# A two-layer post-LN decoder on one core: chunked context reload, a moved key-difference step, per-tile LayerNorm signals and a rebuilt last stage

## The reference

```python
x = ln(x + L0_attn(x))    # linear attention, 16 heads
x = ln(x + L0_xattn(x, ctx))   # softmax attention, 8 heads of 64, over 6404 context rows
x = ln(x + L0_ffn(x))     # mixture of 64 experts, 2 shared ones
x = ln(x + L1_attn(x))    # one softmax head over the 1024 tokens
x = ln(x + L1_xattn(x, ctx))
x = ln(x + L1_ffn(x))

# L1_xattn: every linear layer quantises its input to int8 by its largest magnitude
i_scale = max(max|x|, 1e-8) / 127
out = (clip(round(x / i_scale), -128, 127) @ qW.T) * (w_scale * i_scale) + b
vis, image_embeds = linear(ctx), linear(vis)      # from the context alone
... two attention rounds give `fused` ...
h = relu(linear([fused, mean(image_embeds)], W_f1)); result = linear(h, W_f2)

# L1_ffn: 8 low-rank experts of rank 64, two of them chosen by token 0 for all tokens
gates = softmax over the top 2 of x[0] @ Wr.T
result = x + sum_e gates[e] * (x @ A[e].T) @ Bw[e].T
```

## Time and profile before

| what | us |
|---|---|
| three runs | 1777.51, 1777.84, 1782.12 |
| median | 1777.84 |
| the profiled execution, as timed | 1776.72 |
| its span in the profile | 1775.0 |
| granted TensorE clock, mean | 0.911 of 2.4 GHz |
| layer 0's cross-attention (first exponential to the end of its norm) | 158.3 to 1091.7 |
| pair 3, of this | 884.8 to 1078.4 |
| mixture of experts | to 1328.7 |
| layer 1's cross-attention, first to last exponential | 1460.5 to 1694.1 |
| from its last exponential to the end | 1694.1 to 1775.0 |

### The profile page before, as it was taken

How to read it: one execution, slowest core, us unless ns; L and a number is a source line. 1 busy time by engine, 2 the same in 40 slices (tenths; PEclk the granted TensorE clock), 3 DMA queues, 4 the chain that set the end, 5 groups by cost and what they waited for, 6 DMA issues and landing times.

```text
span 1775.0 us, 26171 instructions
## 1 busy us (share of the span) xinstructions
PE 1532.3 (86%) x8928; PEld 551.9 (31%) x8928; DVE 1289.4 (73%) x2241; ACT 1122.0 (63%) x1495; POOL 424.5 (24%) x411
## 2 busy tenths in 40 slices
PE   3778889999999999999979997999987679968944
PEld 2412223333333333333322323334334413212313
DVE  4698678778787778877759897666655576877764
ACT  4687666776876767867647785555553367655532
POOL 5401333343433334423300010344440000000000
PEclk7957889999999999999989997999997759968967
DMA  4000000000000000000020000111100000000000
GB/s 123 7 0 6 1 1 1 1 1 7 1 1 1 1 1 3 1 1 1 1 58 1 1 1 25 36 43 41 44 13 1 1 1 1 1 0 1 1 1 24
DMA packets 11869, 20.28 MB, mean 11 GB/s; under 512 B 1558, under 2 KB 11046, under 8 KB 11558
## 3 DMA queue, kind: packets, MB, share of 16 engines
q1 hardware_dynamic: 11750, 18.76, 3.9%
HBM read 18.23 MB, written 0.52 MB: 11 GB/s over the span
## 4 chain that ended last, share of the span: by engine, by line
PE 53%; issue 17%; DVE 17%; ACT 7%; POOL 4%; DMA 2%; ACTq 0%; POOLq 0%; SPq 0%; DVEq 0%
PE PS L1704 21%; PE PS L1689 13%; DVE KNB L1049 5%; POOL WRK L575 4%; PE PS L1736 3%; DVE WRK L1099 3%; PE PS L1652 2%; ACT KNB L729 2%; ACT WRK L709 2%; PE PS L1579 2%; DMA KNB<-in_ctx_fm_dram 1%; DVE QS L1105 1%; ACT KB L630 1%; PE PS L1978 1%; DVE KB L979 1%
## 5 line engine op out<-in xcount | busy, mean ns | idle before, releaser
L1099 DVE TENSOR_TENSOR WRK<-WRK 128x768 f32<-128x768 f32 (+1 forms) x500 | 545.0, 1090 | 56.9 <-ACT WRK L709 45.3
L709 ACT ACTIVATE WRK<-PS 128x1024 f32<-128x1024 f32 (+1 forms) x510 | 497.4, 1023 | 105.9 <-PE PS L1689 91.5
L1704 PE MATMUL PS<-WRK,V 128*64 128x512 f32 (+1 forms) x2040 | 498.4, 609 | 0.0
L1049 DVE CUSTOM_DVE_ANT_0 KNB<-PS,KNB 128x512 f16<-128x512 f32 (+2 forms) x464 | 330.9, 730 | 120.1 <-PE PS L1736 108.0
L548 POOL TENSOR_TENSOR WRK<-WRK 128x256 f32<-128x256 f32 x300 | 269.8, 899 | 426.7 <-ACT WRK L709 406.9
L729 ACT ACTIVATE KNB<-PS 128x512 f16<-128x512 f32 (+2 forms) x306 | 181.0, 591 | 121.9 <-PE PS L1736 121.6
L1874 PE MATMUL PS<-WRK,KNB 128*128 128x512 f16 x828 | 196.4, 382 | 11.0 <-POOL WRK L575 4.3
L1689 PE MATMUL PS<-Q,KB 64*128 64x512 f16 (+1 forms) x1428 | 192.3, 381 | 11.3 <-ACT WRK L709 11.2
L1704 PEld LDWEIGHTS PS<-WRK,V 128*64 128x64 f32 (+1 forms) x2040 | 124.4, 136 | 246.5 <-issue 176.8
L1689 PE MATMUL PS<-KNB,KB 64*128 64x512 f16 (+1 forms) x1224 | 152.9, 378 | 0.0
L575 POOL TENSOR_TENSOR WRK<-KB,WRK 128x1024 f16<-128x1024 f32 x46 | 98.6, 2143 | 136.1 <-ACT WRK L850 136.1
(11 more groups left out here) (335 smaller groups left out, 1568.5 us busy)
## 6 DMA issues: line engine op xcount, KB each, us to landing
V<-in_moe_w_dram SPq DMA_DIRECT2D x44, 192.0 KB, 2.4
KNB<-in_ctx_fm_dram SPq DMA_DIRECT2D x1, 2401.5 KB, 18.8
CTX<-in_ctx_fm_dram SPq DMA_DIRECT2D x1, 2401.5 KB, 13.5
BW<-in_bit_w_dram SPq DMA_DIRECT2D x1, 960.0 KB, 6.3
PWK<-in_pair_w_dram SPq DMA_DIRECT2D x4, 192.0 KB, 2.8
SM<-in_small_dram SPq DMA_DIRECT2D x1, 716.5 KB, 4.4
XT<-in_x_fm_dram SPq DMA_DIRECT2D x1, 512.0 KB, 5.2
X<-in_x_tm_dram SPq DMA_DIRECT2D x1, 512.0 KB, 8.0
```

The lines of the kernel that those rows point to most:

```text
L709: e.activation(PR[0:r, u % 2, b, :], bank(2 * b, 2 * b + 2, slice(0, r)), ACT.Exp).then_inc(S("exp"), 1)
L1049: return e.tensor_tensor_reduce(diffs, sums, diffs, 0.5, NEG, ALU.add, ALU.max, accum_out=out)
L1099: e.tensor_tensor(total, total, part, ALU.add).then_inc(S("acc"), 1)
L1704: ins = e.matmul(PS[h * HD:(h + 1) * HD, 4, :], v(r, j, h), PR[0:r, unit_no(hf, i) % 2, b, h * HALF:(h + 1) * HALF], start=(j == 0), stop= ...
```

## The change

It has nine parts. The diff below is cut to its core; renamed semaphores and repeated forms are left out.

1. The context is loaded again in 7 chunks, each as soon as the value projections that read its bytes are done (4, 8, 8, 12, 12, 13 and 13 of pair 3's 13 groups, the last of them in slot 0 of pair 3), ahead of the wait for `r_add`. CHAIN loses two empty entries.
2. The `dk` items stand between the two score tiles on PE and between the two exponentials on ACT. Their DVE part stays.
3. Each of a norm's 8 DVE instructions signals; PE transposes tile by tile, ACT copies in two halves, and some readers start on the first half.
4. The store of the output is two DMAs of 256 KB.
5. W_f1: one DVE pass quantises (no cap at 127 or floor at -128), the second is split by halves between DVE and ACT; the mean is quantised on POOL, multiplied in 4 matmuls of one column, and becomes part of the relu's bias. 16 matmuls over 512 columns become 8.
6. Before W_f2: one DVE pass a block instead of two, the last block converted on DVE; PE goes block by block; DVE adds from PSUM, scaled, to a residue with the bias already in.
7. A and Bw are loaded at the end of the attention, A is transposed there.
8. The top-2 choice is made by `max` and `match_replace`, on 128 partitions.
9. The 8 low-rank experts are made one 128 x 128 matrix (4 matmuls), which the tokens are multiplied by (8 matmuls instead of 8 over 512 columns and 32 over 128).

```diff
+def values_before(c):
+    a, w = KCH[c]
+    last = max(k % NC for k in (2 * a, 2 * (a + w) - 1)) if 2 * (a + w) <= NC or 2 * a >= NC else NC - 1
+    return last // HALF + 1
+RELOAD = sorted(range(NKC), key=values_before)
-CHAIN = [("none",)] * 4
+CHAIN = [("none",)] * 2
 # SP
-                if p:
+                if p and p + 1 < PAIRS:
+                    q.wait_ge(S("r_add"), 2 * p)
+                if p + 1 == PAIRS:
+                    for c in RELOAD:
+                        a, w = KCH[c]
+                        q.wait_ge(S("v_ps"), p * NVG + values_before(c))
+                        q.dma_start(CTX[0:DC, a:a + w], ctx_fm[:, a:a + w]).then_inc(S(f"ld_ctx{c}"), 16)
                     q.wait_ge(S("r_add"), 2 * p)
                 q.dma_start(PWO[:, :], pair_w[p, :, 3, :]).then_inc(S("ld_pwo"), 16)
-            q.wait_ge(S("v_ps"), PAIRS * NVG)
-            q.dma_start(CTX[0:DC, :], ctx_fm).then_inc(S("ld_ctx"), 16)
...
-            q.wait_ge(S("ln_x"), 5)
+            q.wait_ge(S("pv"), unit_no(2 * PAIRS + 1, NU - 1) + 1)
+            q.wait_ge(S("acc"), (2 * PAIRS + 2) * KT)
             q.dma_start(LA, lr_a).then_inc(S("ld_lr"), 16)
...
 # POOL
+                if i == 4:
+                    e.wait_ge(S("ws"), 5)
+                    link(e.tensor_scalar(AVG[:, 0:1], AVG[:, 1:2], AI[:, 4:5], MAGIC, ALU.mult, ALU.add))
+                    e.tensor_scalar(AQ[:, :], AVG[:, 0:1], MAGIC, None, ALU.subtract).then_inc(S("avg_q"), 1)
 # ACT; PE has the same form, with scores in the place of exp
                     exp(hf, i, 0)
                     magnitude(p, mid)
+                    for x in filter(inside, ITEMS[p][s]):
+                        bank5(x)
                     if len(tiles_of(i)) > 1:
                         exp(hf, i, 1)
                     magnitude(p, last)
...
             def to_fm(k, a):
-                e.wait_ge(S("xt_ps"), k)
-                e.activation(XT[:, :], bank(a, a + 2), ACT.Copy).then_inc(S("x_fm"), 1)
+                for h in range(2):
+                    e.wait_ge(S("xt_ps"), 2 * (k - 1) + h + 1)
+                    e.activation(XT[:, h * HALF:(h + 1) * HALF], bank(a + h), ACT.Copy).then_inc(S("x_fm"), 1)
...
+            e.wait_ge(S("lat_ps"), 1)
+            e.activation(LAT, bank(7), ACT.Copy).then_inc(S("lat"), 1)
+            e.wait_ge(S("quant_hi"), 1)
+            e.activation(FQ[:, HALF:T], XF[:, HALF:T], ACT.Identity, bias=NMAG[:, :]).then_inc(S("quant_lo"), 1)
 # DVE
                 for t in range(NT):
-                    ins = e.tensor_scalar(X_[:, t, :], R[:, t, :], LNM[:, t, 0:1], LNR[:, t:t + 1],
-                                          ALU.subtract, ALU.mult)
-                ins.then_inc(S("ln_x"), 1)
+                    e.tensor_scalar(X_[:, t, :], R[:, t, :], LNM[:, t, 0:1], LNR[:, t:t + 1], ALU.subtract,
+                                    ALU.mult).then_inc(S("ln_x"), 1)
...
-            link(quantize(FQ, XT[:, :], XF, 4))
-            link(quantize(AVG[:, 2:3], AVG[:, 1:2], AVG[:, 0:1], 4))
-            e.tensor_copy(AQ, AVG[:, 2:3].to_broadcast([P, HALF])).then_inc(S("quant"), 1)
+            link(e.tensor_scalar(XF, XT[:, :], AI[:, 4:5], MAGIC, ALU.mult, ALU.add))
+            e.sem_inc(S("quant_hi"), 1)
+            e.tensor_scalar(FQ[:, 0:HALF], XF[:, 0:HALF], MAGIC, None, ALU.subtract).then_inc(S("quant"), 1)
+            e.wait_ge(S("cb_ps"), 1)
+            e.scalar_tensor_tensor(CB[:, :], PS[:, 6, 0:4], WS[:, 4:5], sm("b_f1"), ALU.mult, ALU.add
+                                   ).then_inc(S("f1_bias"), 1)
...
             for b in range(4):
-                link(e.tensor_scalar(HB[b], HB[b], AI[:, 5:6], 127.0, ALU.mult, ALU.min))
-                e.tensor_scalar(HB[b], HB[b], -128.0, MAGIC, ALU.max, ALU.add).then_inc(S("h_magic"), 1)
+                e.tensor_scalar(HB[b], HB[b], AI[:, 5:6], MAGIC, ALU.mult, ALU.add).then_inc(S("h_magic"), 1)
+            e.wait_ge(S("h_magic"), 4)
+            e.tensor_scalar(HBQ[3], HB[3], MAGIC, None, ALU.subtract).then_inc(S("h_int3"), 1)
+            for h in range(2):
+                e.wait_ge(S("f2o_ps"), h + 1)
+                part = r2[:, h * HALF:(h + 1) * HALF]
+                ins = e.scalar_tensor_tensor(part, bank(h), WS[:, 5:6], part, ALU.mult, ALU.add)
...
+            link(e.max(best, GL0))
+            e.tensor_scalar(GNM, best[:, 0:1], -1.0, None, ALU.mult).then_inc(S("tail_dve"), 1)
+            link(e.memset(best[:, 2:RE], -NEG))
+            link(e.match_replace(left, best, GL0, NEG))
+            link(e.tensor_scalar(sel, left, NEG, None, ALU.is_equal))
+            e.wait_ge(S("g_exp"), 1)
...
+            for b in range(4):
+                ins = e.tensor_scalar(LBG[:, b, :], LB[:, b, :], GC[:, b:b + 1], None, ALU.mult)
 # PE
+            e.wait_ge(S("avg_q"), 1)
+            for b in range(4):
+                ins = e.matmul(PS[:, 6, b:b + 1], BQ[:, 512 + FFN + b * P:512 + FFN + (b + 1) * P], AQ[:, :], ...)
...
+            for b in range(4):
+                e.wait_ge(S("h_int3" if b == 3 else "h_int"), 1 if b == 3 else b + 1)
+                for t in range(NT):
+                    ins = e.matmul(PS[:, t // 4, ...], HBQ[b][:, t * P:(t + 1) * P], BQ[:, 1536 + b * P: ...], ...)
...
+            e.wait_ge(S("x_fm"), 7)
+            e.matmul(PS[:, 7, 0:RE], XT[:, 0:1].to_broadcast([P, P]), sm("w_r"), ...).then_inc(S("tail_pe"), 1)
+            e.wait_ge(S("tail_dve"), 2)
+            for b in range(4):
+                ins = e.matmul(PS[:, 6, 0:D], LAT[:, b * P:(b + 1) * P], LBG[:, b, :], start=(b == 0), stop=(b == 3))
+            ins.then_inc(S("tail_pe"), 1)
+            e.wait_ge(S("tail_dve"), 3)
+            for t in range(NT):
+                ins = e.matmul(PS[:, 4 + t // 4, ...], XT[:, t * P:(t + 1) * P], LW, start=True, stop=True)
```

261 lines of the change are left out of this document (127 added, 134 removed).

## The result

The changed kernel takes 1726.95 us (median of 4 runs, 1725.69 to 1728.39) against 1777.67 for the kernel before beside it, a ratio of 0.9715 with an interval of 0.9693 to 0.9737. The forecast was 1730.8, with a range from 1720 to 1745. The profiled execution took 1728.0 us, its span is 1726.3.

What follows compares the result with a forecast made beforehand. PE, busy 86%, sets the pace, so time is won where it stands still. Terms 11.8 + 3 + 6.6 + 3.9 - 0.2 + 6.75 + 14.9 + 0.3 = 47.0 us took 1776.72 to 1729.7, median 1730.8; range 1720 to 1745.

Steps and rivals of the forecast that it cites:

- Part 1: Pair 3's context reload: DVE's wait goes and PE gets its stall back; 11.8 us won net, bounds 8 and 12.5.
- Part 2: dk items moved inside slots, pairs 0 to 2: 1 us a half, 3 won; bounds 9 won, 8 lost.
- Rival (b): Pairs 0 to 2: the moved dk copy costs 0.25 us at each slot, 8 lost, 1742 us; chance 0.14.
- (d): All 39 dk slots: ACT's wait for the second score tile delays PE; slower than before, 1782 us; chance 0.02.
- Part 3: Norms by tile: readers start earlier at norms 3, 2 and 1 (2.75, 2.4, 1.45); 6.6 us won, bounds 4 and 8.
- Part 4: W_f1: half quantising passes and fewer matmuls win 3.9 us; the mean on POOL loses 0.2.
- Part 5: W_f2, from the first pass to norm 5's statistics: 13.86 us before, 6.75 us won.
- Part 6: From E, the end of norm 5's last tile, to norm 6's input: E + 11.9 with slow products, 14.9 us won.
- Rival (a): After norm 5, the last products run fast because PE stays at full clock; 3.5 us less, 1727; chance 0.12.
- Rival (e): From norm 5, the path is the gates' chain and not PE; 4 us less is won, 1735; chance 0.05.
- Part 7: Output store in halves: 0.3 us won; the second half still pays most of the landing.
- Rival (c): DVE binds pair 3 once the pause is gone; 8 us won instead of 11.8, 1735; chance 0.06.

Runs made afterwards that it cites:

- experiments 5 and 6: 5: kernel before, whole context transfer issued ahead of the residual wait, 1768.86 us; 6: changed kernel, chunks issued behind it, rounding two slots later, 1727.63 us.
- experiment 4: Changed kernel with PE's transposes waiting for all 8 tiles of each norm; 1733.86 us.
- experiment 3: Changed kernel with the sums of the quantised weights' magnitudes moved earlier, POOL's partition sum right behind its first partition maximum; 1718.10 us.
- experiment 9: Changed kernel with 20 unread filler products on PE, 8 ahead of norm 5's transposes and 12 behind the gate logits; 1724.06 us.

## Why the prediction was right, and where its steps were not

The sum was 47.0 us and 48.7 came: 12.3 + 7.3 + 8.0 - 2.4 + 6.85 + 15.1 + 0.9 for the stages of the seven parts, and 0.7 in layer 1's halves. The close agreement is in part luck: one term was 6.1 too high, and norm 3 alone 3.4 too low.

- **Part 1** (11.8): half 6 won 12.3. The slot's 12.3 and the 0.5 lost in the slot before came as worked out. What I had not said is that the place in the queue does it and not the chunks (experiments 5 and 6).
- **Part 2** (3, "in most dk slots this is a draw; in the four early slots and in those with three micro steps ... 0.3 to 0.7 a slot is won"): the odd halves won 2.4, 2.1 and 2.4, 6.8 in all; the other 0.4 of halves 0 to 5 lie in half 0, which holds no dk item. The draw was right, if over two slots: a late dk slot and its neighbour, 4.45 and 4.86 us before, take 4.75 and 4.48. The four early ones won 0.21, 0.51, 0.22 and 0.22, and two late ones 0.32 and 0.60, which sums to 2.1. I had the right slots and rounded their sum down to 1 us a half. Rival (b), a cost of 0.25 a slot, came in seven of the nine late dk slots (0.24 to 0.30 in half 1), but the slot behind each gave back 0.38 or more, which the rival had not counted. So (b) fell in the sum, and (d) with it.
- **Part 3** (6.6): mis-sized by place. Norm 3 was 2.75 in the sum and is 6.15; I had left out that an earlier start also brings the clock up earlier (experiment 4), and the second half's products overlap the copies. Norm 2 was 2.4: its first readers start 2.8 us earlier, but only 1.0 is left at norm 3, less than that stretch differs between kernels with the same code there (242.6 to 244.7). Norm 1 was 1.45: from its last tile to the first exponential 90.9 became 88.1, 2.8 won, but norm 1 itself ended 1.8 later in this execution, in a stretch that the change leaves alone, so that the table shows 1.0.
- **Part 4** (3.9 - 0.2) is the step that failed, and in it the term for POOL: "I bound it by nothing and by a whole DVE pass, 0.74, and take 0.2 lost". It cost 5.8 us. The stage lost 2.4 instead of winning 3.7. I priced the instruction and not the switch before it. The trace of before had rows for this (experiment 3): POOL's running sums stood for 6 to 7 us on both sides of the reduction in half 0. I looked for POOL in "that form" only, and not for what POOL does after a partition_all_reduce.
- **Part 5** (6.75): 6.85.
- **Part 6** (14.9): 15.1. The four products cost the slow price of the earlier trace rows to the hundredth (2.08); the eight took 3.58, where twice that price is 4.2. The selection and scaling ended at E + 4.85, against 4.6. Rival (a), fast products, needed PE to stay at full clock; the window shows 0.54 of it. The earlier trace rows were slow for the same reason: a window over them gives 0.50. The rule of the Trainium skill (TensorE: Matmul & The Clock Gate, What's actually happening), that an idle array falls to 1.2 GHz, agrees with that window, and experiment 9 with its reverse. Rival (e) did not come.
- **Part 7** (0.3): from the last sum to the end 8.9 became 8.0, so 0.9.
- **Rival (c)** did not come: slots 6 to 11 of pair 3 are at 3.27 us, as most slots around them; slot 12 takes 4.15, which slot 13 took before.

## What to carry to other kernels

Ask of each moved instruction what its engine did just before it: one small POOL instruction behind a partition reduction cost 5.8 us, more than its whole edit was to win (3.7). A MODIFY_POOL_CONFIG in the trace marks the place. When a transfer is late, look first at what stands ahead of it in its queue: the early place alone gave all of the gain, the cutting alone 10.5 of 12.3 us. A step that fills an idle stretch on one engine must be moved on every engine of its chain: half the move cost 5.7 us a half where the whole one won 2.3.

## What the runs showed of the hardware

- On POOL, 5.7 to 7.6 us with the releaser "issue" pass between a partition_all_reduce and a tensor_scalar or tensor_tensor, in both directions (over the thirteen traces 5.7 to 6.6 into a reduction, 6.7 to 7.6 into the others), whether the form had been used before or not. A pair of MODIFY_POOL_CONFIG stands at the head of each. Between two reductions there is neither: in kernel 3 the second starts 0.1 us after its operand. A copy is not enough to bring the pair: POOL's copy at 158.37, behind a reduction, has none, and the tensor_tensor behind the copy pays 6.94.
- Twelve f32 products over 128 columns took 5.7 us with PE idle for 4.1 us before them, at a granted clock of 0.53, and 3.2 us behind filler products at 1.00. The filler paid for itself.
- From norm 2 to norm 3 (the mixture of experts) 245.7 and 247.8 us passed in the kernel before and kernel 5, which do not differ there, and 242.6 to 244.7 in the kernels with the changed norms. That spread stays open.
